# A graph kernel in which GpSimd no longer computes: VectorE splits the weights of both sides

## The chip, the cores and the metric

The kernel runs on one core of a Trainium2 chip. The metric is the device time of one execution in microseconds; less is better. The core's engines run side by side and meet at semaphores: TensorE (PE in the profile, its weight loads PEld), VectorE (DVE), ScalarE (ACT), GpSimd (POOL) and SyncE (SP). Every engine but TensorE and VectorE here also issues transfers between HBM and on-chip memory (SBUF). TensorE accumulates in eight PSUM banks.

## What is computed

Two layers of a graph network over 8192 nodes with 64 features and a dense 0/1 matrix `adj` (8192 x 8192, int32, some 16 neighbours in a row). Layer 0 is a graph attention block of depth 2, layer 1 takes the mean over neighbours:

```python
h = relu(layernorm(x)); outs = [h]
for i in range(2):
    Wh = h @ W[i]
    u, v = Wh @ lin_w[i][:64] @ attn[i], Wh @ lin_w[i][64:] @ attn[i]
    e = leaky_relu(u + v.T + lin_b[i] @ attn[i], 0.2)
    att = softmax(where(adj > 0, e, -9e15), axis=1)
    g = 0.2 * h0 + 0.8 * elu(att @ Wh)      # h0: the first h
    h = g; outs.append(h)
x = x + concat(outs) @ mlp_w + mlp_b
h = relu(layernorm(x)); a = (adj == 1)
out = x + concat([a @ h / a.sum(1), h]) @ weight + bias
```

The output is 8192 x 64, float32.

## The kernel before

The exponential of a leaky ReLU has a kink: for u + v + c over 0 it is exp(u)exp(v), else exp(0.2u)exp(0.2v). So `att @ Wh` becomes two products of 0/1 masks with weights: the on side takes the neighbours over the kink, the off side those under it, each with its own row and column factors. `wsplit` holds the weights Wh times the column factor, split into parts of 16 bits that add up to the float32 value: three bfloat16 parts (195 columns) for the on side, made by `split_on`, and two float16 parts (130 columns) for the off side, made by `split_off`. Both also carry a column of ones for the denominators.

The work is cut into 8 row groups (g) of 1024 rows and 8 chunks (c) of 1024 nodes; n = 8g + c counts these 64 blocks. There are three passes over them. In the first (depth 0) SyncE loads the int32 matrix in halves of 2 MB into three buffers; VectorE turns each half into codes (`convert`, L726) and packs four into a byte (L737, L738, L742); TensorE transposes them (L1302), ScalarE takes them (L470) and stores them to HBM for the later passes. In the second (depth 1) and the third (the mean) the codes are only loaded.

A block of the first two passes is four units q. For each, ScalarE makes a ramp (L462, two instructions) that says which pairs lie over the kink, into one of 8 buffers; VectorE makes from it and the codes the on mask (L706) and the off mask (L714); TensorE multiplies the on mask in 16 matmuls (L1312) and the off mask in 16 (L1318). VectorE's order is written out by hand. In the first pass a block's is: on, on, off, convert, off, on, convert, off, on, pack pairs (2), off, pack, and in row group 0 then the split of the next chunk's on side (L696 to L700). In row groups 1 to 7 steps of the previous group's attention rows take that place. In the second pass the order is on, on, off, off, on, on, off, off, with the same splits in row group 0.

TensorE waits in row group 0, before the first unit of chunk c, for both sides of that chunk: `w_on` and `w_off`.

Before each pass stand the scales. VectorE reduces its maxima (L647), GpSimd takes the maximum over the partitions (`partition_all_reduce`, L327 in the first pass, L344 in the second), VectorE computes the exponents from L656 on, ScalarE takes the exponentials and VectorE finishes (`scl`). In the second pass the order is: last rows of the first pass, one block's masks, scales, splits.

GpSimd's queue, in order: constants and a first all-reduce for the weights; stores of u and x; the all-reduce L327; a load of the scaled input (L305); the eight off-side splits of the first pass (L314 multiply, L315 cast, L316 subtraction, chained by semaphores, through the tile `po`); then transfers only, up to the all-reduce L344; the eight off-side splits of the second pass; then transfers only.

Of the kernel before, what the change touches and what calls it, by code (L numbers as in the profile page):

```python
# [12 lines left out]
ALU = mybir.AluOpType  # L13
# [4 lines left out]
P = 128  # L18
N = 8192
C = 64  # L20
CE = C + 1
# [65 lines left out]
def gnn_program(nc, x, adj, w, lin_w, lin_b, attn, mlp_w, mlp_b, w1, bias1, out):  # L87
    ctx = ExitStack()
    with ctx:
# [98 lines left out]
        def grp(k):  # L188
            return slice(IT * k, IT * k + IT)
# [52 lines left out]
        with nc.Block() as block:  # L242
# [28 lines left out]
            def _(pool):  # L271
# [35 lines left out]
                def split_off(l, c):  # L307
                    ts = grp(c)
                    ch = offch
                    pool.wait_ge(scl, l + 1)  # L310
                    if l == 1:
                        pool.wait_ge(off_sum, 3 * NG)
                    hi, lo = woff[:, ts, WO:WO + CE], woff[:, ts, WO + CE:WO + WF]
                    ch.step(nc.gpsimd.tensor_tensor(po[:, :, :], hw[:, ts, :], expv[:, ts, 1:2].to_broadcast([P, IT, CE]), ALU.mult))  # L314
                    ch.step(nc.gpsimd.tensor_copy(hi, po[:, :, :]))  # L315
                    nc.gpsimd.tensor_tensor(lo, po[:, :, :], hi, ALU.subtract).then_inc(w_off, 1)  # L316
                    pool.wait_ge(w_off, NCH * l + c + 1)

                offch = Chain(pool, och)
# [9 lines left out]
                for c in range(NCH):  # L329
                    split_off(0, c)  # L330
# [30 lines left out]
                for c in range(NCH):  # L361
                    split_off(1, c)
# [176 lines left out]
            def _(dve):  # L539
                ec = Chain(dve, ech)  # L540
                bc = Chain(dve, bch)
                sc = Chain(dve, sch)
                lc = Chain(dve, lch)
# [157 lines left out]

                def on_mask(l, n, q):
                    U = LU * l + 4 * n + q
                    dve.wait_ge(sgn, U + 1)
                    on = w32(onb[U % NS])
                    nc.vector.scalar_tensor_tensor(on, on, word(BITS[q]), w32(pt[(NT * l + n) % NP]), ALU.bitwise_and,  # L706
                                                   ALU.bitwise_and).then_inc(on_r, 1)
# [133 lines left out]
                split_on(0, 0)  # L841
                convert(1, 1)
                pack_pairs(1)
                pack(1)
                for n in range(NT):
# [41 lines left out]
                    if g == 0 and r + 1 < NCH:  # L887
                        split_on(0, r + 1)
                    if g > 0 and r == 0:
                        row_scales(g - 1)  # L890
# [36 lines left out]
                split_on(1, 0)  # L927

# [112 lines left out]
                for n in range(NT):  # L1041
# [57 lines left out]
                    if g == 0 and r + 1 < NCH:  # L1099
                        split_on(1, r + 1)  # L1100
                    if g > 0:
# [475 lines left out]
```

## Time and profile before

| | |
|---|---|
| median of three runs | 1882.42 us (1879.76 to 1882.54) |
| the profiled execution | 1880.38 us, span 1878.6 us |
| TensorE busy | 1552.6 us, 83% of the span |
| VectorE busy | 1598.8 us, 85% |
| ScalarE busy | 1230.0 us, 65% |
| GpSimd busy | 147.3 us, 8% |
| moved | 353.91 MB, 188 GB/s over the span |

The first pass runs from about 160 to 970 us, the turn to the second up to 1012, the second to about 1620 and the mean after it. Busy shares over the whole span mix these; the rows further down are by stage. Where an instruction's time overlaps with its successor's, the distance from start to start says what it costs its engine. The granted clock is a share of TensorE's full 2.4 GHz; 0.5 is its lower level, 1.2 GHz.

### The profile page before, as it was taken

The page shows a single profiled execution, that of the slowest core. Times are in us where ns is not written, and L with a number is a line of the kernel's source. Part 1 is how long each engine was busy: PE and PEld are TensorE (multiplying, and loading weights), DVE is VectorE, ACT ScalarE, POOL GpSimd, SP SyncE. Part 2 cuts the span into 40 slices and gives each one's busy share as a digit, 9 for nine tenths or more (in the row PEclk, how much of TensorE's full clock was granted, in tenths as well). Part 3 has the DMA queues.
Part 4 walks back from the last instruction along what each step waited for, and adds up shares of the span by engine and source line. Part 5 has one row for each costly group of instructions (what it writes and reads, how often), then busy time and mean ns, then how long its engine had stood idle before and what let it go on. Part 6 is the DMA issues. An engine that isn't in the chain of part 4 may idle for free. (4 is left out here: it accounts for less than half of the span.)

```text
span 1878.6 us, 50382 instructions
## 1 busy us (share of the span) xinstructions
PE 1552.6 (83%) x21780; PEld 1500.3 (80%) x21780; DVE 1598.8 (85%) x2697; ACT 1230.0 (65%) x1269; POOL 147.3 (8%) x162
## 2 busy tenths in 40 slices
PE   0223788888888888888874999999999999899998
PEld 0122777877878787878764999999999999889998
DVE  1669999999999999999986976886977968987675
ACT  0335576878877787778856899999999999000000
POOL 0017100000000000000005100000000000000000
PEclk9956889999999999999986999999999999999999
DMA  7128789999999999999921111111212101133231
GB/s 192 56 46 297 280 319 353 380 354 373 376 366 388 360 384 353 397 347 409 343 91 23 52 53 35 52 42 58 58 39 66 53 24 52 41 86 109 85 97 48
DMA packets 130912, 353.91 MB, mean 188 GB/s; under 512 B 25217, under 2 KB 33409, under 8 KB 130689
## 3 DMA queue, kind: packets, MB, share of 16 engines
q1 hardware_dynamic: 90240, 304.10, 43.6%
q0 software_dynamic: 7936, 25.24, 5.4%
q10 hardware_dynamic: 32512, 21.34, 3.9%
q8 instruction: 171, 2.80, 0.6%
q14 instruction: 53, 0.43, 0.1%
HBM read 323.32 MB, written 27.33 MB: 187 GB/s over the span
## 5 line engine op out<-in xcount | busy, mean ns | idle before, releaser
L462 ACT ACTIVATE region<-ub,bigv 128x1024 uint8<-128x1024 f32 x1024 | 1098.2, 1142 | 54.7 <-PE bank L1312 22.1
L1312 PE MATMUL bank<-wsplit,region 128*128 128x195 bf16 x8192 | 789.1, 250 | 86.3 <-DVE region L706 47.2
L1312 PEld LDWEIGHTS bank<-wsplit,region 128*128 128x128 fp8e3 x8192 | 692.0, 99 | 103.5 <-issue 47.9
L1318 PE MATMUL bank<-wsplit,region 128*128 128x130 f16 x8192 | 564.4, 223 | 66.3 <-DVE region L714 65.4
L1318 PEld LDWEIGHTS bank<-wsplit,region 128*128 128x128 fp8e3 x8192 | 505.8, 99 | 96.4 <-DVE region L714 94.8
L714 DVE SCALAR_TENSOR_TENSOR region<-region 128x512 uint32<-128x512 uint32 x512 | 347.1, 695 | 24.1 <-PE bank L1318 23.4
L706 DVE SCALAR_TENSOR_TENSOR region<-region 128x512 uint32<-128x512 uint32 x512 | 343.4, 699 | 1.4 <-ACT region L462 1.3
L726 DVE TENSOR_SCALAR region<-region 128x4096 uint8<-128x4096 int32 x128 | 294.4, 2301 | 0.9 <-DMA region<-in_adj 0.8
L1506 PE MATMUL bank<-wsplit,region 128*128 128x129 f16 x4096 | 242.9, 221 | 11.4 <-DVE region L1148 11.4
L1506 PEld LDWEIGHTS bank<-wsplit,region 128*128 128x128 fp8e3 x4096 | 240.7, 98 | 12.8 <-DVE region L1148 12.8
L470 ACT ACTIVATE region<-bank 128x1024 uint16<-128x1024 uint16 x64 | 65.3, 1021 | 134.0 <-PE bank L1302 133.4
L1148 DVE TENSOR_SCALAR region<-region 128x512 uint32<-128x512 uint32 x256 | 100.4, 424 | 43.1 <-PE bank L1506 37.6
L1268 PE MATMUL bank<-identh,hcat 128*128 128x128 f16 x256 | 23.1, 243 | 78.3 <-DVE hcat L594 77.4
L1268 PEld LDWEIGHTS bank<-identh,hcat 128*128 128x128 f16 x256 | 18.2, 109 | 80.5 <-issue 74.6
L292 POOL DMA_DIRECT2D u_d<-uu x16 | 14.2, 885 | 770.1 <-DVE pmx L612 770.1
L1302 PE MATMUL bank<-identb,region 128*128 128x128 bf16 x512 | 40.6, 224 | 30.0 <-DVE region L742 23.6
L763 DVE TENSOR_REDUCE parts<-bank 128x130 f32<-128x390 f32 x64 | 34.1, 558 | 31.6 <-PE bank L1312 29.1
L1302 PEld LDWEIGHTS bank<-identb,region 128*128 128x128 bf16 x512 | 32.6, 100 | 30.6 <-DVE region L742 24.0
L478 ACT ACTIVATE po<-po 128x512 f32<-128x512 f32 x16 | 10.0, 624 | 53.9 <-DVE po L805 53.9
L742 DVE SCALAR_TENSOR_TENSOR region<-region 128x512 uint32<-128x512 uint32 x64 | 45.1, 705 | 0.0
L737 DVE SCALAR_TENSOR_TENSOR region<-region 128x512 uint32<-128x512 uint32 x64 | 45.1, 704 | 0.1
L738 DVE SCALAR_TENSOR_TENSOR region<-region 128x512 uint32<-128x512 uint32 x64 | 44.3, 692 | 0.0
(156 smaller groups left out, 775.7 us busy)
## 6 DMA issues: line engine op xcount, KB each, us to landing
region<-in_adj SPq DMA_DIRECT2D x128, 2048.0 KB, 10.9
region<-codes_d SPq DMA_DIRECT2D x128, 256.0 KB, 2.7
codes_d<-region ACTq DMA_DIRECT2D x64, 256.0 KB, 5.9
ub<-u_d POOLq DMA_DIRECT2D x16, 512.0 KB, 5.0
hg<-h_d POOLq DMA_DIRECT2D x16, 256.0 KB, 5.3
region<-in_x SPq DMA_DIRECT2D x8, 256.0 KB, 5.5
h_d<-hg ACTq DMA_DIRECT2D x8, 256.0 KB, 2.0
x_d<-region POOLq DMA_DIRECT2D x8, 256.0 KB, 4.7
```

What stands on the lines that cost most here:

```text
L462: last = nc.scalar.activation(sv[:, b, :], ub[G % 2][:, :], ACT.Relu, bias=bigv[l][:, t:t + 1], scale=BIG)
L470: nc.scalar.activation(pt[n % NP].bitcast(U16), tpb[:, :].bitcast(U16), ACT.Copy).then_inc(p_in, 1)
L706: nc.vector.scalar_tensor_tensor(on, on, word(BITS[q]), w32(pt[(NT * l + n) % NP]), ALU.bitwise_and, ALU.bitwise_and).then_inc(on_r, 1)
L714: nc.vector.scalar_tensor_tensor(w32(offb[U % NO]), w32(pt[(NT * l + n) % NP]), word(BITS[q]), w32(onb[U % NS]), ALU.bitwise_and, ALU.bitw ...
L726: nc.vector.tensor_scalar(code[:, 4 * h:4 * h + 4, :], adjb[m % NA], 1.375, 3.0, ALU.mult, ALU.min).then_inc(coded, 1)
L737: nc.vector.scalar_tensor_tensor(pk, cq[1], 2, cq[0], ALU.logical_shift_left, ALU.bitwise_or).then_inc(pairs_r, 1)
L742: nc.vector.scalar_tensor_tensor(pk, hp, 4, pk, ALU.logical_shift_left, ALU.bitwise_or).then_inc(packed_r, 1)
L1148: nc.vector.tensor_scalar(w32(onb[V % NS]), w32(xb[i % 2]), word(BITS[q]), None, ALU.bitwise_and).then_inc(eq, 1)
L1302: last = nc.tensor.transpose(tpb[:, :].bitcast(BF16)[:, it * P:(it + 1) * P], src[:, it, :], identb[:, :])
L1312: return nc.tensor.matmul(acc_on[it], columns(onb[U % NS], it, b), wsplit[:, c * TC + 2 * q + b, 0:WC], start=(c == 0 and q == 0 and b == ...
L1318: return nc.tensor.matmul(acc_off[it], columns(offb[U % NO], it, b), woff[:, c * TC + 2 * q + b, WO:WO + WF], start=(c == 0 and q == 0 and ...
L1506: last = nc.tensor.matmul(acc_m[g % 2][it], columns(onb[V % NS], it, b), wf16[:, c * TC + 2 * q + b, :], start=(first and b == 0 and it % ...
```

## The change

`split_off` moves from GpSimd's block to VectorE's. It has the same three operations on the same tiles. VectorE runs it for each chunk directly after that chunk's `split_on`, in both passes, with a semaphore chain of its own. GpSimd keeps the memory sets, the constants, the three all-reduces and its transfers. The waits of TensorE and of ScalarE are as before.

```diff
@@ gpsimd
-                def split_off(l, c):
-                    ts = grp(c)
-                    ch = offch
-                    pool.wait_ge(scl, l + 1)
-                    if l == 1:
-                        pool.wait_ge(off_sum, 3 * NG)
-                    hi, lo = woff[:, ts, WO:WO + CE], woff[:, ts, WO + CE:WO + WF]
-                    ch.step(nc.gpsimd.tensor_tensor(po[:, :, :], hw[:, ts, :], expv[:, ts, 1:2].to_broadcast([P, IT, CE]), ALU.mult))
-                    ch.step(nc.gpsimd.tensor_copy(hi, po[:, :, :]))
-                    nc.gpsimd.tensor_tensor(lo, po[:, :, :], hi, ALU.subtract).then_inc(w_off, 1)
-                    pool.wait_ge(w_off, NCH * l + c + 1)
...
                 load_h0(0)
-                for c in range(NCH):
-                    split_off(0, c)
                 load_h0(1)
...
-                for c in range(NCH):
-                    split_off(1, c)
                 load_x(0)
@@ vector
+                def split_off(l, c):
+                    ts = grp(c)
+                    hi, lo = woff[:, ts, WO:WO + CE], woff[:, ts, WO + CE:WO + WF]
+                    dve.wait_ge(scl, l + 1)
+                    if l == 1 and c == 0:
+                        dve.wait_ge(off_sum, 3 * NG)
+                    if c > 0 or l > 0:
+                        dve.wait_ge(w_off, NCH * l + c)
+                    oc.step(nc.vector.tensor_tensor(po[:, :, :], hw[:, ts, :], expv[:, ts, 1:2].to_broadcast([P, IT, CE]), ALU.mult))
+                    oc.step(nc.vector.tensor_copy(hi, po[:, :, :]))
+                    nc.vector.tensor_tensor(lo, po[:, :, :], hi, ALU.subtract).then_inc(w_off, 1)
...
                 split_on(0, 0)
+                split_off(0, 0)
                 convert(1, 1)
...
                     if g == 0 and r + 1 < NCH:
                         split_on(0, r + 1)
+                        split_off(0, r + 1)
...
                 split_on(1, 0)
+                split_off(1, 0)
...
                     if g == 0 and r + 1 < NCH:
                         split_on(1, r + 1)
+                        split_off(1, r + 1)
```

In the changed kernel the line numbers are lower by 16 from `split_on` on (L696 becomes L680) and, after the new function, by 4 (L706 becomes L702); the new `split_off` stands at L694 to L696, and the second pass's all-reduce at L329.

GpSimd at the turn between the passes, before. DMA rows are transfers; an ISA row without tiles is one that the compiler put in, an ISA row with `hmx` is the all-reduce:

```order
L337 DMA m_d<-stg 128x8x64
L305 DMA hg<-h_d 128x512 [waits h_ready,h0_stored1]
L344 ISA
L344 ISA hmx<-hmx 128x2 [waits max_parts]
L314 ISA
L314 TENSOR_TENSOR po<-hw,expv 128x520 [waits off_sums_done,scaled]
L315 CAST wsplit<-po 128x8x65 [waits off_chain]
```

And after:

```order
L322 DMA m_d<-stg 128x8x64
L305 DMA hg<-h_d 128x512 [waits h_ready,h0_stored1]
L329 ISA hmx<-hmx 128x2 [waits max_parts]
L339 DMA stg<-x_d 128x8x64 [waits m1_stored0,m1_stored1,x0_stored,v_u_ready]
L340 DMA stg<-m_d 128x8x64
```

The arithmetic is gone, and with it both ISA rows without tiles, the one ahead of the all-reduce and the one ahead of the first multiply; in the first pass likewise the one ahead of its first multiply.

VectorE at the second pass's start, before, from the end of the scales over the first chunk's split to the start of the second's:

```order
L684 TENSOR_SCALAR rowf<-rowf,hsc 128x64 [waits scale_chain]
L696 TENSOR_TENSOR av<-hw,expv 128x520 [waits row_chain,on_side_split,on_sums_done,scaled]
L697 CAST wsplit<-av 128x8x65 [waits split_chain]
L698 TENSOR_TENSOR bb<-av,wsplit 128x520 [waits split_chain]
L699 CAST wsplit<-bb 128x8x65 [waits split_chain]
L700 TENSOR_TENSOR wsplit<-bb,wsplit 128x8x65 [waits split_chain]
L696 TENSOR_TENSOR av<-hw,expv 128x520 [waits on_side_split,row_chain,scaled]
```

And after:

```order
L668 TENSOR_SCALAR rowf<-rowf,hsc 128x64 [waits scale_chain]
L680 TENSOR_TENSOR av<-hw,expv 128x520 [waits row_chain,on_side_split,on_sums_done,scaled]
L681 CAST wsplit<-av 128x8x65 [waits split_chain]
L682 TENSOR_TENSOR bb<-av,wsplit 128x520 [waits split_chain]
L683 CAST wsplit<-bb 128x8x65 [waits split_chain]
L684 TENSOR_TENSOR wsplit<-bb,wsplit 128x8x65 [waits split_chain]
L694 TENSOR_TENSOR po<-hw,expv 128x520 [waits off_side_split,off_sums_done,scaled]
L695 CAST wsplit<-po 128x8x65 [waits off_chain]
L696 TENSOR_TENSOR wsplit<-po,wsplit 128x8x65 [waits off_chain]
L680 TENSOR_TENSOR av<-hw,expv 128x520 [waits on_side_split,row_chain,scaled]
```

Three operations stand behind each of the eight on-side splits of a pass, 48 in all. TensorE's and SyncE's rows are the same in both kernels.

## Rows read from the trace of the kernel before

**Rows 1.** Stages: us, each engine's busy us (count), TensorE's granted clock, transfers' share, GB/s

```profile
192.00:262.00 70.00, 53.52 (x673) 51.68 (x672) 69.31 (x93) 44.88 (x44) 2.47 (x1) 0.91 0.82 315
262.00:980.00 718.00, 607.77 (x8038) 564.68 (x8036) 710.01 (x933) 559.47 (x582) 29.45 (x29) 0.98 0.94 352
1012.00:1046.00 34.00, 30.75 (x393) 30.00 (x394) 33.62 (x36) 26.01 (x25) 27.80 (x23) 0.93 0.12 33
1046.00:1600.00 554.00, 554.00 (x7908) 554.00 (x7906) 443.74 (x826) 515.55 (x480) 22.00 (x31) 1.00 0.17 48
```

**Rows 2.** VectorE's waits from 262 to 980 us: us in total, times, longest us

```profile
DVE parts L763 <- PE bank L1312: 5.6, 1, 5.6
DVE region L726 <- DMA region<-in_adj: 0.8, 2, 0.5
```

**Rows 3.** Timeline of GpSimd, first pass: start, us, instruction [idle before <-releaser]

```profile
144.74 0.72 POOL L327 PARTITION_ALL_REDUCE hmx<-hmx  x1
...
156.21 1.83 POOL L314 TENSOR_TENSOR po<-hw,expv 128x520 f32<-128x520 f32 x1 [10.32 <-issue]
...
190.12 1.47 POOL L316 TENSOR_TENSOR wsplit<-po,wsplit 128x520 f16<-128x520 f32 x1
```

**Rows 4.** Timeline of VectorE: conversions and first masks of chunks

```profile
154.84 2.29 DVE L726 TENSOR_SCALAR region<-region 128x4096 uint8<-128x4096 int32 x1
...
161.09 2.56 DVE L706 SCALAR_TENSOR_TENSOR region<-region 128x512 uint32<-128x512 uint32 x2
...
188.02 2.56 DVE L706 SCALAR_TENSOR_TENSOR region<-region 128x512 uint32<-128x512 uint32 x2
...
218.72 1.28 DVE L706 SCALAR_TENSOR_TENSOR region<-region 128x512 uint32<-128x512 uint32 x2
...
220.53 2.29 DVE L726 TENSOR_SCALAR region<-region 128x4096 uint8<-128x4096 int32 x1
222.73 0.68 DVE L714 SCALAR_TENSOR_TENSOR region<-region 128x512 uint32<-128x512 uint32 x1
...
232.76 1.28 DVE L706 SCALAR_TENSOR_TENSOR region<-region 128x512 uint32<-128x512 uint32 x2
```

**Rows 5.** Timeline of VectorE: an on-side split beside which GpSimd is idle

```profile
215.71 0.69 DVE L696 TENSOR_TENSOR av<-hw,expv 128x520 f32<-128x520 f32 x1
216.44 0.43 DVE L697 CAST wsplit<-av 128x520 bf16<-128x520 f32 x1
216.90 0.70 DVE L698 TENSOR_TENSOR bb<-av,wsplit 128x520 f32<-128x520 f32 x1
...
218.10 0.70 DVE L700 TENSOR_TENSOR wsplit<-bb,wsplit 128x520 bf16<-128x520 f32 x1
```

**Rows 6.** Timeline of all engines at the turn and the second pass's start

```profile
992.53 0.57 POOL L305 DMA_DIRECT2D hg<-h_d  x1
...
1001.01 0.37 POOL L344 PARTITION_ALL_REDUCE hmx<-hmx  x1 [7.91 <-issue]
1001.42 0.16 DVE L656 TENSOR_TENSOR cv<-hmx,cb 128x1 f32<-128x1 f32 x1 [10.62 <-POOL hmx L344]
...
1008.42 1.44 DVE L700 TENSOR_TENSOR wsplit<-bb,wsplit 128x520 bf16<-128x520 f32 x1
...
1010.41 1.48 POOL L316 TENSOR_TENSOR wsplit<-po,wsplit 128x520 f16<-128x520 f32 x1
...
1012.25 2.77 PE L1312 MATMUL bank<-wsplit,region 128*128 128x195 bf16 x16 [23.60 <-POOL wsplit L316]
```

**Rows 7.** Timeline of TensorE, second pass: waits for masks, and two undisturbed units

```profile
1034.42 1.51 PE L1312 MATMUL bank<-wsplit,region 128*128 128x195 bf16 x16 [1.41 <-DVE region L706]
...
1045.43 1.51 PE L1312 MATMUL bank<-wsplit,region 128*128 128x195 bf16 x16 [0.17 <-DVE region L706]
...
1049.97 1.51 PE L1312 MATMUL bank<-wsplit,region 128*128 128x195 bf16 x16
...
1052.24 1.51 PE L1312 MATMUL bank<-wsplit,region 128*128 128x195 bf16 x16
```

More of the change, by code:

```diff
@@ L305, in load_h0 @@
                     pool.dma_start(hg[E % 2][:, :, :], dgrp(h0_d, E % NG)).then_inc(hg_in[E % 2], 16)
-                def split_off(l, c):
-                    ts = grp(c)
-                    ch = offch
-                    pool.wait_ge(scl, l + 1)
-                    if l == 1:
-                        pool.wait_ge(off_sum, 3 * NG)
-                    hi, lo = woff[:, ts, WO:WO + CE], woff[:, ts, WO + CE:WO + WF]
-                    ch.step(nc.gpsimd.tensor_tensor(po[:, :, :], hw[:, ts, :], expv[:, ts, 1:2].to_broadcast([P, IT, CE]), ALU.mult))
-                    ch.step(nc.gpsimd.tensor_copy(hi, po[:, :, :]))
-                    nc.gpsimd.tensor_tensor(lo, po[:, :, :], hi, ALU.subtract).then_inc(w_off, 1)
-                    pool.wait_ge(w_off, NCH * l + c + 1)
-                offch = Chain(pool, och)
                 for k in range(NG):
@@ L542, in _ @@
                 sc = Chain(dve, sch)
+                oc = Chain(dve, och)
                 lc = Chain(dve, lch)
```

## The prediction

> **What bounds the kernel now.** I read the busy times by engine first, then the same by stages, then the waits, and last the timeline where GpSimd computes. VectorE is the busiest engine over the span, but an average over the two passes hides that they have different limits [rows 1]. In the first pass (the matrix is read, coded and used) VectorE is busy 710.01 of 718 us and TensorE 607.77: VectorE sets the pace. Its only waits there are 5.6 us for TensorE at the pass's end and 0.8 us for the matrix's transfers [rows 2]. In the second pass TensorE is busy 554.00 of 554 us at full clock and VectorE only 443.74. So work taken off VectorE pays in full in the first pass and nothing in the second, except where TensorE waits: at the turn between the passes, and in the second pass's first eight chunks.
>
> **The change part by part.** The off-side split of one chunk is a multiply, a cast and a subtraction. Eight chunks go from GpSimd to VectorE in each pass.
>
> (a) Added to VectorE, first pass. The same shapes stand in the on-side split, undisturbed, start to start: multiply 215.71 to 216.44, 0.73 us; cast to 216.90, 0.46; last subtraction 218.10 to the next mask at 218.72, 0.62 [rows 4, 5]. The new group costs 1.81 us, eight of them 14.5 us. Nothing covers it, since VectorE is the bound: +14.5. The float16 output instead of bfloat16 has the same width, so I take the price without a margin.
>
> (b) Taken from VectorE, first pass: its own slow stretch. GpSimd splits from 156.21 to 191.59 [rows 3]. From one chunk's first mask to the next one's an undisturbed chunk takes 218.72 to 232.76, 14.04 us. The chunk of 161.09 to 188.02 took 26.93 with the same instructions: 12.9 too much. The next two, 188.02 to 218.72, took 30.70 against 28.08 and 0.41 for three small operations that only they have (L747, L751, L756): 2.2 too much. Before them, from the conversion at 154.84 to 161.09, stand 6.25 us for a conversion, 2.20 undisturbed (220.53 to 222.73), and three packing operations, which like the masks take 0.60 each where two in a row take 1.28 with the overlap: 4.0 in all, 2.25 too much. VectorE is never idle in it; its instructions themselves are longer, from just after GpSimd's first start until its last end [rows 3, 4]. Together 17.4 us. They go if VectorE runs alone: -17.4. First pass net: -2.9.
>
> What could be late next there? The first masks: VectorE's extra 1.81 us comes before them, but 2.25 goes, so TensorE starts at about the same time, 160.7 for 161.1. The matrix's transfers: a chunk will need its 4 MB every 15.9 us instead of every 14.0, which asks less of them. TensorE needs some 9.7 us for a chunk at full clock (four units of 2.27, 1049.97 to 1052.24 [rows 7], and a transpose), so it waits a little longer for each chunk. I let -2.9 stand at the pass's end, where VectorE's only long wait is for TensorE, which itself follows the masks.
>
> (c) The turn. At 990.8 VectorE has the partial maxima and begins to wait, 10.62 us. GpSimd issues its last transfer at 992.53 and is free at 993.10, yet its all-reduce starts at 1001.01, after 7.91 us in which it waits for nothing that the profile shows [rows 6]; VectorE, ScalarE and TensorE stand still meanwhile. In the first pass the all-reduce followed the same kind of transfer with no idle time [rows 3]. What differs is in the order of GpSimd's rows: in the kernel before an extra ISA row stands ahead of the second all-reduce, and one ahead of each pass's first multiply, where in the first pass 10.32 us of such idle time stand [rows 3]. In the changed kernel all three are gone, since GpSimd never changes from the all-reduce to arithmetic and back. Bounds: nothing (the pause has another cause) and 7.9. I take 7.9, because the same instruction without that row paid nothing: -7.9. GpSimd's remaining transfers keep their order; the second load of the scaled input only moves from behind the split to ahead of it.
>
> The Trainium skill, GPSIMD Engine Reference, section 2.1, puts the first call to freshly loaded GpSimd code at about 6 us without a visible instruction. An estimate by that page is -6.0 in place of -7.9, 2 us less gain; the trace's own pause is longer and I go by it.
>
> (d) The second pass's start. TensorE starts at 1012.25, released by GpSimd's last subtraction of the first chunk, which ends at 1011.89 [rows 6]. In the changed kernel VectorE does that chunk after its own, whose last subtraction started at 1008.42: 0.62 for it, then 1.81, so 1010.9, and about 0.1 more to TensorE. That is 1.2 us earlier: -1.2.
>
> (e) The second pass's first eight chunks. Here too VectorE is slow while GpSimd computes (the last subtraction of the first split takes 1.44 us where 0.70 is the undisturbed one [rows 5, 6]), and TensorE waits three times for masks, 3.0 us in all, the first 1.41 and the last 0.17 us [rows 7]. After: VectorE needs 8 masks of 0.60 and two splits of 3.0 and 1.8 for a chunk, 9.6 us; TensorE needs 4 x 2.27, 9.1. VectorE loses 0.5 us for a chunk but starts with a lead: its masks for the third chunk are due about 1026, TensorE wants them about 1032. Over five more chunks the lead shrinks from 6 to about 3 us and then the splits end. So the waits go: -3.0. Bounds: 0, if the lead is less than I count, and -3.0. From 1046 on TensorE is never idle, so what is gained by then stays until the end.
>
> Sum: -2.9 - 7.9 - 1.2 - 3.0 = **-15.0 us**. Against the profiled execution's own 1880.38 that is 1865.4. The median of the three runs is 2.0 higher, 1882.42, and 15.0 off it gives 1867.4. I predict **1867**.
>
> **The rivals.**
> A: as worked out, 1867.
> B: the first pass gives nothing back, because something else, the transfers first, takes over when VectorE is faster: the transfer engines are busy 0.94 of that pass [rows 1]. For it: that share. Against it: 0.8 us of waits for them in all [rows 2]. 12.1 off: 1870.
> C: the pause before the all-reduce stays. For it: it shows as idle time without a releaser, and its cause is read from the order of rows alone. Against it: the first all-reduce. 7.1 off: 1875.
> D, slower: the long VectorE instructions are not GpSimd's doing but the place's. Then (a) is paid and (b) does not come, +14.5, the turn gives -7.9, and (d) and (e) nothing: +6.6, 1889. The forecast turns to a loss once less than 2.4 of the 17.4 us come back. For it: many transfers start in the same stretch. Against it: the second pass shows the same long instructions beside GpSimd with the transfer engines almost idle (0.12 busy from 1012 to 1046 [rows 1]), and they end with GpSimd's work both times.
> The Trainium skill, Perfetto Trace Analysis, section Optimizing Scalar/DVE Operations, advises to offload from a saturated DVE, even to GPSIMD, which speaks against this change; it adds that it "might not help" between these two, as they share a port. The trace's 17.4 against 14.5 us sides with the addition.
> E, about level or slower: TensorE's clock. With a longer wait for each chunk of the first pass's first eight it may stay at 1.2 GHz. Its first 16 matmuls after the turn take 2.77 us, the same 16 later 1.51 [rows 6, 7], 1.83 times; a chunk of 9.7 us becomes 17.8, and then TensorE, not VectorE at 15.9, sets the pace: 1.9 x 8 = +15 on -15.0, 1882, no change, and slower with any lag on top. The whole gain is gone only if all of TensorE's work there runs low; the granted clock of 192 to 262 us is 0.91 [rows 1], so I give it little.
>
> **How the numbers follow.** A 0.77, B 0.08, C 0.07, E 0.03, D 0.05. A's own ends: (e) at 0 instead of -3.0, and the two references 1880.4 and 1882.4 for the sum, give 1865 to 1870, and runs differ by 1 to 3 us. The range takes in B and leaves out C, D and E: **1862 to 1874**. About 0.2%, 3.8 us, is what a measurement of this kernel can tell from no change. A, B and C are beyond it: faster 0.92; E, within it, 0.03; D, slower, 0.05.
>
> **What would show it.** In the changed kernel's profile: VectorE's first masks of chunks one and two 15.9 us apart instead of 26.9, and of later chunks of that group 15.85 instead of 14.04; the wait for the all-reduce at the turn about 2.7 us instead of 10.6, and no idle time without a releaser ahead of it; TensorE's start 1.2 us closer to VectorE's last on-side subtraction; no wait for masks in the second pass's first eight chunks. The end of the first pass should be 2.9 us earlier and all later points 11 to 15. Wrong would be: VectorE's operations still 1 to 1.6 us long with GpSimd idle (D), the pause still there (C), waits for the matrix's transfers (B), a granted clock under 0.6 between 190 and 260 us (E).

## The result, and the profile after

The changed kernel took 1865.61 us, median of 4 runs (1864.2 to 1868.48), against 1881.81 us for the kernel before (4 runs, 1879.76 to 1882.54): a ratio of 0.9918, 95% interval 0.99 to 0.9935, so 16.2 us less. The forecast was 1867. The profiled execution took 1868.48 us with a span of 1866.6, the longest of its four runs, and 12.0 us under the span of before.

The same stages as in [rows 1], in the same columns (length, busy time of TensorE's matmuls, of its weight loads, of VectorE, ScalarE and GpSimd with counts, granted clock, transfers' share, GB/s):

```profile
192.00:262.00 70.00, 50.76 (x595) 48.73 (x596) 69.14 (x94) 45.18 (x43) 2.20 (x1) 0.83 0.69 265
262.00:980.00 718.00, 606.24 (x7999) 564.33 (x7997) 707.29 (x931) 555.06 (x577) 28.73 (x27) 0.97 0.94 351
1012.00:1046.00 34.00, 34.00 (x482) 34.00 (x480) 33.21 (x58) 32.61 (x31) 0.00 (x0) 1.00 0.12 33
1046.00:1600.00 554.00, 554.00 (x7906) 554.00 (x7905) 444.61 (x827) 504.45 (x470) 21.87 (x31) 1.00 0.16 48
```

GpSimd's column of 1012 to 1046 us is now 0 and TensorE works all 34 of those us, where it had 30.75. In the stretch of 192 to 262 us TensorE's granted clock is lower, 0.83 for 0.91: it is busy 50.76 of the 70 us there, for 53.52. VectorE's waits from 262 to 980 us, as in [rows 2]:

```profile
DVE parts L759 <- PE bank L1312: 5.6, 1, 5.6
DVE region L722 <- DMA region<-in_adj: 3.5, 4, 1.6
```

It waited 3.5 us for the matrix's transfers instead of 0.8. GpSimd in the first pass, as in [rows 3], now has the all-reduce and two loads there and then nothing for 112 us:

```profile
144.60 0.72 POOL L314 PARTITION_ALL_REDUCE hmx<-hmx  x1
145.19 1.10 POOL L305 DMA_DIRECT2D hg<-h_d  x2
258.37 2.20 POOL L299 DMA_DIRECT2D ub<-u_d  x1 [112.08 <-ACT region L445]
```

VectorE's first chunk, which answers to [rows 4 and 5]. The conversion at 156.60, the first masks of chunks 0, 1 and 2, and the off-side split in its new place:

```profile
156.60 2.29 DVE L722 TENSOR_SCALAR region<-region 128x4096 uint8<-128x4096 int32 x1
...
160.86 1.29 DVE L702 SCALAR_TENSOR_TENSOR region<-region 128x512 uint32<-128x512 uint32 x2
...
174.90 0.70 DVE L694 TENSOR_TENSOR po<-hw,expv 128x520 f32<-128x520 f32 x1
175.63 0.43 DVE L695 CAST wsplit<-po 128x520 f16<-128x520 f32 x1
176.09 0.70 DVE L696 TENSOR_TENSOR wsplit<-po,wsplit 128x520 f16<-128x520 f32 x1
176.71 1.29 DVE L702 SCALAR_TENSOR_TENSOR region<-region 128x512 uint32<-128x512 uint32 x2
...
192.76 1.29 DVE L702 SCALAR_TENSOR_TENSOR region<-region 128x512 uint32<-128x512 uint32 x2
```

From first mask to first mask it is 15.85 us (160.86 to 176.71), where [rows 4] had 26.93; the split takes 1.81 (174.90 to 176.71). At the turn, as in [rows 6]:

```profile
992.70 0.57 POOL L305 DMA_DIRECT2D hg<-h_d  x1
993.29 0.31 POOL L329 PARTITION_ALL_REDUCE hmx<-hmx  x1
993.63 0.16 DVE L640 TENSOR_TENSOR cv<-hmx,cb 128x1 f32<-128x1 f32 x1 [2.68 <-POOL hmx L329]
...
1000.87 0.70 DVE L684 TENSOR_TENSOR wsplit<-bb,wsplit 128x520 bf16<-128x520 f32 x1
...
1002.68 0.70 DVE L696 TENSOR_TENSOR wsplit<-po,wsplit 128x520 f16<-128x520 f32 x1
...
1003.75 2.77 PE L1312 MATMUL bank<-wsplit,region 128*128 128x195 bf16 x16 [14.94 <-DVE wsplit L696]
```

The all-reduce starts 0.02 us after GpSimd's last transfer, with no idle time without a releaser. VectorE waits 2.68 us for it, not 10.62, and TensorE is released by VectorE's subtraction of the off side. TensorE has no wait for masks in the second pass's first eight chunks, which [rows 7] had three times.

One thing of the kernel before went unread in the prediction. Behind its all-reduce GpSimd was idle once more, ahead of the first multiply of its splits, and the end of this was on the way to TensorE's start:

```profile
1006.02 0.70 DVE L696 TENSOR_TENSOR av<-hw,expv 128x520 f32<-128x520 f32 x1
1008.11 1.19 POOL L314 TENSOR_TENSOR po<-hw,expv 128x520 f32<-128x520 f32 x1 [6.73 <-issue]
```

Most of the 6.73 us went by while the scales were made, but VectorE's own split, which needs the same scales, began 2.1 us before GpSimd's. The change removes this delay as well; the prediction has its effect inside step (d), which counts from GpSimd's last subtraction.

### The profile page after: what moved, and what is told of

Its sections match the earlier page's. It is cut to its first block and busy times, and to the rows that moved or that the text cites. A ratio compares the mean times of both kernels' runs of the same rounds, so it can differ in the third digit from the quotient of the medians.

```text
span 1866.6 us, 50375 instructions
## 1 busy us (share of the span) xinstructions
PE 1554.5 (83%) x21780; PEld 1505.2 (81%) x21780; DVE 1593.7 (85%) x2745; ACT 1230.2 (66%) x1269; POOL 83.3 (4%) x114
## 5 line engine op out<-in xcount | busy, mean ns | idle before, releaser
L710 DVE SCALAR_TENSOR_TENSOR region<-region 128x512 uint32<-128x512 uint32 x512 | 340.8, 683 | 24.1 <-PE bank L1318 23.4
L702 DVE SCALAR_TENSOR_TENSOR region<-region 128x512 uint32<-128x512 uint32 x512 | 334.8, 683 | 1.4 <-ACT region L445 1.3
L1506 PE MATMUL bank<-wsplit,region 128*128 128x129 f16 x4096 | 243.2, 222 | 11.6 <-DVE region L1148 11.6
L1506 PEld LDWEIGHTS bank<-wsplit,region 128*128 128x128 fp8e3 x4096 | 241.2, 99 | 12.8 <-DVE region L1148 12.8
L292 POOL DMA_DIRECT2D u_d<-uu x16 | 14.1, 883 | 775.2 <-DVE pmx L596 775.2
L733 DVE SCALAR_TENSOR_TENSOR region<-region 128x512 uint32<-128x512 uint32 x64 | 43.7, 683 | 0.1
L738 DVE SCALAR_TENSOR_TENSOR region<-region 128x512 uint32<-128x512 uint32 x64 | 43.7, 683 | 0.0
L1137 DVE SCALAR_TENSOR_TENSOR region<-region 128x512 uint32<-128x512 uint32 x64 | 43.7, 683 | 0.0
```

What stands on the lines that cost most here:

```text
L710: nc.vector.scalar_tensor_tensor(w32(offb[U % NO]), w32(pt[(NT * l + n) % NP]), word(BITS[q]), w32(onb[U % NS]), ALU.bitwise_and, ALU.bitw ...
L733: nc.vector.scalar_tensor_tensor(pk, cq[1], 2, cq[0], ALU.logical_shift_left, ALU.bitwise_or).then_inc(pairs_r, 1)
L738: nc.vector.scalar_tensor_tensor(pk, hp, 4, pk, ALU.logical_shift_left, ALU.bitwise_or).then_inc(packed_r, 1)
L1506: last = nc.tensor.matmul(acc_m[g % 2][it], columns(onb[V % NS], it, b), wf16[:, c * TC + 2 * q + b, :], start=(first and b == 0 and it % ...
```

## The experiments

I cut each trace at two marks: VectorE's reduction of its maxima ahead of a pass (139.82 and 990.62 us in the kernel before) and TensorE's first matmul of the second pass (1012.25). Between the first two lies the first pass, between the last two the turn, behind them the rest. The last column is VectorE's whole wait for the matrix's transfers. The kernel before was timed anew with each group of runs (medians 1881.54, 1881.53 and 1881.75 us); the changed kernel was not, so differences from its 1865.61 can be off by a few tenths of a us from that, besides the spread of the runs. The profiled executions gave, in us:

| kernel | first pass | turn | rest | wait for the matrix |
|---|---|---|---|---|
| before | 850.8 | 21.6 | 866.4 | 0.8 |
| changed | 851.1 | 13.0 | 862.9 | 3.5 |
| first_only | 849.5 | 14.2 | 865.7 | 2.1 |
| second_only | 851.2 | 22.4 | 861.8 | 1.4 |
| early_reduce | 851.5 | 14.3 | 866.5 | 1.4 |
| tiny_arith | 847.9 | 21.8 | 861.9 | 0.7 |
| side_reads | 865.3 | 21.8 | 861.7 | 1.6 |
| side_writes | 849.6 | 12.9 | 862.5 | 0 |
| half_before | 849.6 | 22.5 | 866.0 | 0 |
| half_after | 847.0 | 12.8 | 863.3 | 0 |
| twice_first | 863.3 | 13.1 | 862.9 | 0.7 |
| twice_second | 848.9 | 14.7 | 873.7 | 1.3 |
| reduce_first | 847.7 | 11.2 | 862.7 | 0.4 |
| reduce_first_late_off | 849.2 | 9.1 | 862.2 | 2.0 |

### One pass at a time: first_only and second_only

`first_only` has VectorE's splits in the first pass and GpSimd's in the second:

```diff
+                for c in range(NCH):
+                    split_off(1, c)
                 load_x(0)
...
                 split_on(1, 0)
-                split_off(1, 0)
...
                         split_on(1, r + 1)
-                        split_off(1, r + 1)
```

> VectorE splits the off side in the first pass alone; in the second GpSimd does, as before. My theory: the first pass gives +14.5 - 17.4 = -2.9 us, the pause before the second all-reduce goes (-7.9) because GpSimd has done no arithmetic since the first one, and (d) and (e) stay as in the kernel before: -10.8, about 1871. If the first pass's gain is eaten by waits for the matrix's transfers: -7.9, about 1874. If the pause has nothing to do with GpSimd's arithmetic: -2.9, about 1879.

Measured: 1871.11 us (1870.23 to 1871.43, 5 runs) against 1881.54, ratio 0.9948 (0.9935 to 0.996): 10.4 less, as the first theory had it to 0.4 us. Its turn is 7.5 us shorter, its first pass 1.3; of the 2.9 expected there, 2.6 came if each pass is taken less its own wait for the matrix (2.1 and 0.8 us).

`second_only` is the reverse:

```diff
                 load_h0(0)
+                for c in range(NCH):
+                    split_off(0, c)
                 load_h0(1)
...
                 split_on(0, 0)
-                split_off(0, 0)
...
                         split_on(0, r + 1)
-                        split_off(0, r + 1)
```

> VectorE splits the off side in the second pass alone; in the first GpSimd does, as before. My theory: the pause of 7.9 us stays, since GpSimd computed before that all-reduce; TensorE starts 1.2 us earlier after VectorE's scales and its three waits of 3.0 us in all go: -4.2, about 1878. If the waits for masks stay, because VectorE has more to do there: -1.2 or less, about 1881.

Measured: 1876.57 us (1875.57 to 1877.06, 10 runs), ratio 0.9974 (0.9965 to 0.9983): 5.0 less, where 4.2 was expected. The first pass is the old one. The two parts of the expectation did not both come: the rest of the run is 4.6 us shorter (861.8 for 866.4, expected 3.0), but the turn is no shorter, 22.4 us for 21.6, where 1.2 less was expected. The pause stands there, since GpSimd had computed in the first pass, and it was 1.0 us longer. GpSimd also goes straight on to issue two transfers, and beside them VectorE's scales, from the first to the next mask, take 2.56 us (1002.65 to 1005.21) instead of 1.89 in the kernel before. The all-reduce, the second of the stretched operations, and TensorE's start:

```profile
1002.24 0.37 POOL L345 PARTITION_ALL_REDUCE hmx<-hmx  x1 [8.91 <-issue]
...
1002.95 0.61 DVE L659 TENSOR_SCALAR expv<-vv,hmx 128x64 f32<-128x64 f32 x1
...
1013.20 2.77 PE L1326 MATMUL bank<-wsplit,region 128*128 128x195 bf16 x16 [24.33 <-DVE wsplit L712]
```

### The pause: early_reduce and tiny_arith

`early_reduce` is the kernel before with a spare all-reduce behind the first pass's splits:

```diff
                 for c in range(NCH):
                     split_off(0, c)
+                pool.wait_ge(dumr, 1)
+                nc.gpsimd.partition_all_reduce(dum[:, 1, :], dum[:, 0, :], P, RMAX).then_inc(dumr, 1)
                 load_h0(1)
```

> The kernel before, with one more all-reduce over a spare tile directly behind GpSimd's eight splits of the first pass, where GpSimd has nothing to do for 70 us. My theory: the change from arithmetic to the all-reduce is paid there, unseen, and the real all-reduce at the turn starts at once: -7.9, about 1874, with all else as before. If the pause belongs to the place (the transfers ahead of it, or the long time since the last all-reduce): no change, 1882.

Measured: 1873.35 us (1872.73 to 1874.66, 5 runs), ratio 0.996 (0.9947 to 0.9974): 8.2 less, from the spare all-reduce alone. The all-reduce at the turn, and VectorE's wait for it:

```profile
993.78 0.31 POOL L349 PARTITION_ALL_REDUCE hmx<-hmx  x1
994.13 0.16 DVE L661 TENSOR_TENSOR cv<-hmx,cb 128x1 f32<-128x1 f32 x1 [2.69 <-POOL hmx L349]
```

So the pause isn't the place's. `tiny_arith` is the reverse, in the changed kernel:

```diff
                 load_h0(0)
+                pool.wait_ge(scl, 1)
+                pool.wait_ge(dumr, 1)
+                nc.gpsimd.tensor_tensor(dum[:, 1, :], dum[:, 0, :], dum[:, 0, :], ALU.add).then_inc(dumr, 1)
                 load_h0(1)
```

> The changed kernel, with one addition of 2 elements per partition on GpSimd in the first pass, into a spare tile. My theory: it brings the pause back, 7.9 us over the changed kernel's 1865.6, 1873.5. By the page of the skill, which puts the first call to newly loaded code at about 6 us: 1871.6. If the pause needs the eight long splits, or comes from the place: 1865.6.

Measured: 1874.4 us (1873.52 to 1876.7, 5 runs), 8.8 over the changed kernel. One addition of two elements per partition, 850 us earlier, brings back the whole pause:

```profile
998.81 0.37 POOL L335 PARTITION_ALL_REDUCE hmx<-hmx  x1 [8.41 <-issue]
...
999.21 0.16 DVE L646 TENSOR_TENSOR cv<-hmx,cb 128x1 f32<-128x1 f32 x1 [11.12 <-POOL hmx L335]
```

So what decides is whether GpSimd did arithmetic since the last all-reduce, and not how much of it. In the five kernels that have it the idle time was 7.91, 8.91, 8.41, 8.36 and 8.30 us (before, second_only, tiny_arith, side_reads, half_before). The Trainium skill (GPSIMD Engine Reference, section 2.1) gives about 6 us, without a visible instruction, for the first call to freshly loaded code. The traces agree in that no instruction stands for the pause; it is longer here, 8.4 us on the mean, and that code is loaded in it is not shown by any trace of this case.

### What lengthens VectorE's instructions: side_reads and side_writes

Both are the changed kernel; GpSimd works in the first pass beside VectorE, into the tile `hg1`, which is loaded anew afterwards.

```diff
...
+                for c in range(NCH):
+                    nc.gpsimd.tensor_tensor(spf, hw[:, grp(c), 0:C], expv[:, grp(c), 1:2].to_broadcast([P, IT, C]), ALU.mult).then_inc(gch, 1)
...
+                    nc.gpsimd.tensor_copy(sph[:, 0, :, :], hw[:, grp(c), 0:C]).then_inc(gch, 1)
...
+                    nc.gpsimd.tensor_tensor(sph[:, 1, :, :], hw[:, grp(c), 0:C], sph[:, 0, :, :], ALU.subtract).then_inc(gdn, 1)
```

> The changed kernel, and in the first pass GpSimd also does the old arithmetic (8 times multiply, cast, subtract, on 512 elements per partition in place of 520), into a tile that nobody reads before it is loaded anew. VectorE's work is the same as in the changed kernel. My theory: VectorE's long instructions come back beside it, about 17 us, and the pause before the second all-reduce, 7.9: 1865.6 + 25, about 1890. If the long instructions are the place's and not GpSimd's: the pause alone, 1873.5, and they would then also have been seen in the changed kernel.

Measured: 1890.49 us (1889.95 to 1891.92, 4 runs), 24.9 over the changed kernel, as expected, and slower than the kernel before: ratio 1.0052 (1.0036 to 1.0069). The first pass is 16.2 us longer than the mean of the six kernels with the new first pass and no stretch of GpSimd work beside it (849.1: changed, first_only, tiny_arith with its one addition, twice_second, reduce_first, reduce_first_late_off). GpSimd's work ends at 192.2 us, and from 192.70 on the masks take 0.68 us again. VectorE's masks and its conversion:

```profile
164.75 1.60 DVE L723 SCALAR_TENSOR_TENSOR region<-region 128x512 uint32<-128x512 uint32 x1
166.27 3.14 DVE L735 TENSOR_SCALAR region<-region 128x4096 uint8<-128x4096 int32 x1
169.33 1.09 DVE L723 SCALAR_TENSOR_TENSOR region<-region 128x512 uint32<-128x512 uint32 x1
170.34 1.61 DVE L715 SCALAR_TENSOR_TENSOR region<-region 128x512 uint32<-128x512 uint32 x1
```

`side_writes` has this in the same place:

```diff
+                for c in range(NCH):
+                    for k in range(8):
+                        nc.gpsimd.memset(spf, 0.0).then_inc(gdn, 1)
```

Measured: 1867.5 us (1866.16 to 1868.83, 4 runs). GpSimd's row, and VectorE beside it:

```profile
151.32 52.86 POOL L323 MEMSET hg<- 128x512 f32 x64 [5.98 <-DVE rowf L678]
```

```profile
165.75 0.68 DVE L712 SCALAR_TENSOR_TENSOR region<-region 128x512 uint32<-128x512 uint32 x1
166.35 2.65 DVE L732 TENSOR_SCALAR region<-region 128x4096 uint8<-128x4096 int32 x1
168.93 0.67 DVE L720 SCALAR_TENSOR_TENSOR region<-region 128x512 uint32<-128x512 uint32 x1
...
173.26 0.59 DVE L691 CAST wsplit<-av 128x520 bf16<-128x520 f32 x1
...
182.61 0.68 DVE L712 SCALAR_TENSOR_TENSOR region<-region 128x512 uint32<-128x512 uint32 x1
183.21 2.58 DVE L732 TENSOR_SCALAR region<-region 128x4096 uint8<-128x4096 int32 x1
```

The masks, with two inputs in on-chip memory, stay at 0.60 us from start to start (165.75 to 166.35, 182.61 to 183.21); the conversions take 2.25 to 2.58 instead of 2.20, the casts 0.53 to 0.68 for 0.43, but for one of 0.44. So what holds up the two-input instructions, to 1.1 to 1.6 us for the row's 0.68, is something that `side_reads` does and the fills don't, reading on-chip memory or computing; the two runs can't tell these apart. The fills leave those instructions alone and lengthen the one-input ones a little, which costs the first pass 2.2 us (849.6 without any wait for the matrix, for 847.4 in the six kernels less their waits). The fills are held up themselves: in the 2.58 us of the conversion at 166.35 GpSimd's trace has 2 of them, in the 3.60 us of masks and packing behind it 7. The Trainium skill (SBUF — State Buffer, section Who interferes with whom) says that it is the reading: a VectorE instruction with two inputs there contends with a GpSimd instruction that reads, not with one that only writes. The trace agrees, with mask rows of 1.60 against 0.68 us. `side_writes` had no pause at the turn (12.9 us): a fill doesn't bring it back.

### The transfers: half_before and half_after

Only half of each matrix tile's columns is loaded from the fourth transfer on, so the codes of the rest are stale; all engines' instructions stay.

```diff
-                    sp.dma_start(adjb[m % NA], adj_v[g, h, :, :, c * CHJ:(c + 1) * CHJ]).then_inc(adj_in[m % NA], 16)
+                    w = CHJ if m < NA else CHJ // 2
+                    sp.dma_start(adjb[m % NA][:, :, 0:w], adj_v[g, h, :, :, c * CHJ:c * CHJ + w]).then_inc(adj_in[m % NA], 16)
```

> The kernel before, but from the fourth transfer on only half of each matrix tile's columns is loaded (1 MB in place of 2), so the codes of the other half are old ones. Every engine's instructions are unchanged. If VectorE alone sets the first pass's pace: within 2 us of the kernel before, 1881. If transfers hold it up at times: 0.8 us of waits go, and what else they cost.

> The changed kernel with the same halved transfers. The changed kernel's profiled run lost in waits for the matrix what it had gained in the first pass (3.5 us of waits against 0.8). If that is the transfers' doing: without them the first pass ends 2.9 us earlier than in the kernel before, and the time is 15 to 16 us under the halved kernel before, with waits of VectorE for transfers near 0. If VectorE's gain was lost otherwise: 12 us under it.

Measured: 1879.55 us (1878.79 to 1880.5, 10 runs) and 1863.38 us (1862.62 to 1864.96, 4 runs): 16.2 apart, and each some 2 us under its full kernel. The first passes are 849.6 and 847.0 us: 2.6 apart with no wait for transfers in either. With the full matrix the wait differs from run to run: 0.8 to 1.4 us in the three traces with the old first pass (before, second_only, early_reduce), 0.4 to 3.5 in the six with the new one. The passes average 851.2 and 849.1 us. Less its own wait each of the three is 849.8 to 850.1 us and each of the six 847.2 to 847.6, again 2.6 apart. So the gain of the first pass is real, and the changed kernel's profiled execution lost it to its 3.5 us of waiting; why that execution waited longest stays open.

### The prices: twice_first and twice_second

Each off-side split of one pass is done twice over, with the same result. `twice_first` is shown; `twice_second` has `l == 1` in the added line.

```diff
+                    for _ in range(1 if l == 0 else 0):
+                        oc.step(nc.vector.tensor_tensor(po[:, :, :], hw[:, ts, :], expv[:, ts, 1:2].to_broadcast([P, IT, CE]), ALU.mult))
+                        oc.step(nc.vector.tensor_copy(hi, po[:, :, :]))
+                        oc.step(nc.vector.tensor_tensor(lo, po[:, :, :], hi, ALU.subtract))
```

> The changed kernel, in which VectorE does each off-side split of the first pass twice over, with the same result. It prices step (a) by itself. If VectorE is the first pass's bound and the group costs 1.81 us: +14.5 on the changed kernel's 1865.6, 1880.1. If part of it hides behind transfers or TensorE: less; the whole of it hidden would be 1865.6.

Measured: 1880.63 us (1878.49 to 1883.41, 11 runs), 15.0 over the changed kernel, and a first pass of 863.3 us, 14.2 over the mean of 849.1 and 15.2 when each is taken less its waits. Expected were 14.5: nothing of it hides.

> The changed kernel with the splits of the second pass done twice. It tests the count of VectorE's lead in step (e). My theory: TensorE starts 1.8 us later, and a chunk then asks 11.45 us of VectorE against TensorE's 9.08; the lead of about 2 us that is left at the third chunk is gone at the fourth, and four more chunks lose 2.4 each: 1.8 + 0.3 + 9.5 = +11.6, 1877.2. If VectorE has more room than I count: +1.8 alone, 1867.4.

Measured: 1879.7 us (1878.18 to 1882.04, 11 runs), 14.1 over the changed kernel where 11.6 was expected. TensorE's first waits for masks:

```profile
1034.80 1.51 PE L1316 MATMUL bank<-wsplit,region 128*128 128x195 bf16 x16 [1.35 <-DVE region L706]
...
1046.37 1.51 PE L1316 MATMUL bank<-wsplit,region 128*128 128x195 bf16 x16 [2.33 <-DVE region L706]
...
1057.95 1.93 PE L1316 MATMUL bank<-wsplit,region 128*128 128x195 bf16 x16 [2.33 <-DVE region L706]
1059.67 1.94 PE L1322 MATMUL bank<-wsplit,region 128*128 128x130 f16 x16
1061.40 1.95 PE L1316 MATMUL bank<-wsplit,region 128*128 128x195 bf16 x16
...
1069.53 1.51 PE L1316 MATMUL bank<-wsplit,region 128*128 128x195 bf16 x16 [0.70 <-DVE region L706]
...
1081.10 1.51 PE L1316 MATMUL bank<-wsplit,region 128*128 128x195 bf16 x16 [2.33 <-DVE region L706]
```

The first wait comes at the fourth chunk (1034.80), as counted. From there VectorE sets the pace: the chunks start 11.57 us apart, and the five waits sum to 9.0 us (1.35, 2.33, 2.33, 0.70, 2.33). The rest of the run is 10.8 us longer than the changed kernel's, the turn 1.7, so 12.5 by stages; the other 1.6 us between the two medians isn't explained. After the wait that ends at 1057.95 three groups of 16 matmuls take 1.93, 1.94 and 1.95 us instead of 1.51, 1.08 and 1.51. The granted clock of the three is 0.77, 0.50 and 0.75: the middle one runs wholly at the lower level, the others in part. It is 5.24 us from 1057.95 to the group at 1063.19 for an undisturbed 3.62. The 1.6 us lost cost nothing more, since the next wait is that much shorter, 0.70. So the lead that step (e) counted is real and is used up by one more split a chunk.

### A version beyond both: reduce_first and reduce_first_late_off

`reduce_first` moves GpSimd's second all-reduce ahead of its last three transfers:

```diff
                     X = NG + e
+                    if e == NG - 1:
+                        pool.wait_ge(vm, 2)
+                        nc.gpsimd.partition_all_reduce(hmx[:, 1, :], hmx[:, 0, :], P, RMAX).then_inc(vall, 1)
                     store_u(X)
...
-                pool.wait_ge(vm, 2)
-                nc.gpsimd.partition_all_reduce(hmx[:, 1, :], hmx[:, 0, :], P, RMAX).then_inc(vall, 1)
```

> The changed kernel with GpSimd's second all-reduce ahead of the last three transfers in its queue (the stores of u and of the mlp part and a load), not behind them. VectorE waited 2.68 us for the all-reduce in the changed kernel's profile, of which the three transfers' issue is 2.2. Expected: about 0.4 us of wait, -2.2, 1863.4. If one of the transfers is then late for someone: less or nothing.

Measured: 1864.15 us (1863.06 to 1865.98, 4 runs), 1.5 under the changed kernel; ratio to before 0.9909 (0.9895 to 0.9923). The turn is 11.2 us, 1.8 shorter, where 2.2 were expected.

`reduce_first_late_off` has in addition, on TensorE:

```diff
                         pe.wait_ge(w_on, NCH * l + c + 1)
-                        pe.wait_ge(w_off, NCH * l + c + 1)
...
                     last.then_inc(on_done, 1)
+                    if g == 0 and q == 0:
+                        pe.wait_ge(w_off, NCH * l + c + 1)
                     pe.wait_ge(off_r, U + 1)
```

> The same, and TensorE waits for a chunk's off-side weights only before its off-side matmuls, not before the on-side ones. At the start of the second pass the on-side matmuls of the first unit take 2.77 us, longer than the off-side split of 1.81: TensorE starts 1.8 us earlier. Expected -4.0 on the changed kernel, 1861.6. In the first pass VectorE sets the pace and nothing changes.

Measured: 1862.62 us (1861.28 to 1865.15, 4 runs), 3.0 under the changed kernel and 0.9903 of the kernel before (0.9888 to 0.9918). The ranges of the two and of the changed kernel overlap, so the order of the three by run times isn't certain; the turn, which is what was changed, is 9.1 us for 13.0, 3.9 less where 4.0 were expected. The all-reduce, VectorE's wait for it, the off side's first multiply and TensorE, which starts beside it:

```profile
989.13 0.35 POOL L323 PARTITION_ALL_REDUCE hmx<-hmx  x1 [10.39 <-DVE hmx L632]
...
989.51 0.16 DVE L641 TENSOR_TENSOR cv<-hmx,cb 128x1 f32<-128x1 f32 x1 [0.48 <-POOL hmx L323]
...
997.61 0.69 DVE L695 TENSOR_TENSOR po<-hw,expv 128x520 f32<-128x520 f32 x1
...
997.91 2.77 PE L1313 MATMUL bank<-wsplit,region 128*128 128x195 bf16 x16 [11.02 <-issue]
```

In both kernels GpSimd issues its transfers directly behind the all-reduce, beside VectorE's scales. Two of these take 0.48 and 0.35 us there instead of 0.25, another 0.51 instead of 0.20, and the scales as a whole, up to the next mask, 2.27 us (989.51 to 991.78) instead of 1.90 in the changed kernel (993.63 to 995.53). That is the 0.4 us that `reduce_first` fell short of its 2.2.

## Why the prediction was right

The forecast was 15.0 us less, 1867 from the median; 1865.6 was measured, within 1862 to 1874, and rival A's mechanism was found at each of its steps.

(a) +14.5. The group took 1.81 us in the changed kernel, and doing it twice cost 15.0 in run time and 14.2 in the first pass.

(b) -17.4. The first two chunks' periods fell from 26.93 and 16.47 to 15.85 and 16.05 us. `side_reads` put the long instructions back, with 16.2 us, which excludes rival D.

(a) and (b) together, -2.9 predicted: -2.6 with the transfers out of the way, -2.6 with the waits taken off, -2.1 on the mean of the profiled executions as they are. Rival B seems to describe the one profiled execution of the changed kernel (first pass 0.3 us longer, waits of 3.5). Taking each pass less its own wait, 847.6 and 850.0 us, would have shown the gain even in that pair.

(c) -7.9. The wait for the all-reduce fell by 7.94, and rival C is excluded from both sides, by `early_reduce` and `tiny_arith`. The pause itself averages 8.4 us, but what its loss gives to the run is 8.0: from VectorE's second mark to the end it is 888.25 us with the pause and 880.28 without where GpSimd splits in the second pass (means of two kernels each), and 883.81 and 875.81 where VectorE does (of three and four).

(d) -1.2. In the recorded pair TensorE's start came 0.95 us closer to VectorE's last on-side subtraction, 2.88 us behind its start (1000.87 to 1003.75) for 3.83 (1008.42 to 1012.25); the step from VectorE's last subtraction to TensorE was 0.45 us, not the 0.1 of the prediction. Between kernels without a pause ahead of the all-reduce TensorE starts at 14.2 us from the mark with GpSimd's second-pass splits and at 12.9 with VectorE's: 1.3. With the pause in place there was nothing to gain: 22.0 us with VectorE's splits (second_only, tiny_arith, side_reads) for 22.1.

(c) and (d) together, -9.1 predicted: the turn is 22.1 us (mean of before and half_before) and 12.9 (of four kernels like the changed one), -9.1.

(e) -3.0. The three waits are gone. The rest of the run is 866.1 us in the mean of four kernels with GpSimd's second-pass splits and 862.5 in eight with VectorE's: -3.7. Most of the additional 0.7 is in how the waits were priced. In the kernel before, the first of them:

```profile
1031.92 1.09 PE L1318 MATMUL bank<-wsplit,region 128*128 128x130 f16 x16
1034.42 1.51 PE L1312 MATMUL bank<-wsplit,region 128*128 128x195 bf16 x16 [1.41 <-DVE region L706]
```

The idle time is 1.41 us, but from start to start it is 2.50 where 0.92 is the undisturbed step: 1.58 lost, since one group's 1.09 us reaches past the start of the next. Priced in this way the three waits cost 3.5 us in the kernel before, not 3.0, and 3.5 to 3.9 in the other three kernels with GpSimd's splits, 3.7 on the mean. The two families don't differ by this alone: by TensorE's 31st on-side group (1086.33 before, 1074.52 after) they are 3.3 us apart on the mean. TensorE's first groups, at the lower clock level, lose between 1.2 and 2.7 us from run to run, and 0.4 more on the mean where VectorE splits. The 0.4 us that come behind the 31st group stay open.

Stage by stage that is -2.1 - 9.1 - 3.7 = -14.9. With the waits for the matrix taken off, and the pause apart, it is -2.6 for the first pass, -8.0 for the pause and -4.4 for (d) and (e) together, -15.0, where the steps were -2.9, -7.9 and -4.2. So the sum wasn't right by luck: no term was off by more than 0.3 us, (d) and (e) taken as one. On 1881.5 to 1881.8 either gives 1867; the medians of the two kernels are 16.2 apart, inside what their interval allows (12 to 19 us).

Rival E was given little for the right reason: the granted clock fell to 0.83 in 192 to 262 us, with each chunk's first groups at the lower level (2.77 us at 177.54 and 225.48 us), but TensorE at 2.4 GHz for the rest of each kept within VectorE's 15.9 us.

## What to carry to other kernels

Work that a helper engine does "for nothing" can cost the bound engine more than doing it itself: compare the bound engine's instruction times inside and outside the helper's stretch before believing in the offload, here 17.4 us lost against 14.5 us of work saved. An idle gap on GpSimd without a releaser ahead of an all-reduce was, in every trace here, behind arithmetic; keep arithmetic off GpSimd between two all-reduces, or put a spare all-reduce where nobody waits. One profiled execution of a stage that runs at the edge of its transfers can be off by as much as the effect sought: cut several traces at the same marks, and take each one's own waits off, which here left 0.4 us of spread. And price a wait of TensorE from start to start, not by its idle time.

## What the runs showed of the hardware

The pause of GpSimd before an all-reduce that follows arithmetic was 7.9 to 8.9 us at the turn, after one addition of two elements as after the 24 instructions of eight splits; 64 fills of memory didn't cause it (`side_writes`, turn 12.9 us). The other way, from the all-reduce to the first multiply, GpSimd was idle for 6.73 us at the turn of the kernel before and started 2.1 us behind VectorE's split, which needs the same scales.

GpSimd's arithmetic, which reads on-chip memory, stretched VectorE's two-input masks from 0.68 us to between 1.09 and 1.61 (`side_reads`). GpSimd's fills left them alone and stretched conversions from 2.20 us to between 2.25 and 2.58, while only 2 fills fell into a conversion of 2.58 us where 7 fell into 3.60 us of masks (`side_writes`). GpSimd's issue of transfers stretched VectorE's scales from 1.90 us to 2.27 (`reduce_first_late_off`) and 2.56 (`second_only`).

In `twice_second` TensorE waited 2.33 us three times between the same amounts of work; behind one of them the granted clock fell to 0.50 for a group of matmuls, behind the others the groups kept their 1.51 us.
